# Pointwise products and forward row transform of the spectral layers, split into halves of 64 stationary columns

## What is computed

```python
def _spectral_conv(x, w1, w2):
    xf = jnp.fft.rfft2(x).reshape(Bb, G, WID, Hh, Wf)
    lo = jnp.einsum('bgixy,gioxy->bgoxy', xf[:, :, :, :M1, :M2], w1c)
    hi = jnp.einsum('bgixy,gioxy->bgoxy', xf[:, :, :, Hh - M1:, :M2], w2c)
    ...
    return jnp.fft.irfft2(out_ft.reshape(Bb, G * WID, Hh, Wf), s=(Hh, Ww))
h = _gconv1x1(h, fc0_w, fc0_b)
for i in range(4):
    h1 = _spectral_conv(h, sp_w1[i], sp_w2[i])
    h2 = _gconv1x1(h, w_w[i], w_b[i])
    h = h1 + h2
    if i < 3:
        h = _gswish(h, betas[i])
h = _gswish(_gconv1x1(h, fc1_w, fc1_b), betas[3])
return _gconv1x1(h, fc2_w, fc2_b)
```

## Time and profile before

| | |
|---|---|
| median of 3 runs | 3073.56 us |
| the profiled execution | 3098.2 us, its span 3096.2 us |
| mean granted TensorE clock | 0.92 of full speed |
| TensorE busy (matmul) | 2572.4 us, 83% of the span |
| TensorE weight loads busy | 1994.0 us, 64% |
| VectorE / ScalarE / GpSimd busy | 1935.2 / 1290.9 / 1026.9 us |
| the layers | from 1110 to about 2440 us of the span |

### The profile page before, as it was taken

How to read it: one execution, slowest core, us unless ns; L and a number is a source line. 1 busy time by engine, 2 the same in 40 slices (tenths; PEclk the granted TensorE clock), 3 DMA queues, 4 the chain that set the end, 5 groups by cost and what they waited for, 6 DMA issues and landing times. The chain is left out here.

```text
span 3096.2 us, 46908 instructions
## 1 busy us (share of the span) xinstructions
PE 2572.4 (83%) x18156; PEld 1994.0 (64%) x18156; DVE 1935.2 (63%) x2352; ACT 1290.9 (42%) x2167; POOL 1026.9 (33%) x1050
## 2 busy tenths in 40 slices
PE   0499999685978768999899989898987599999468
PEld 0144444343655457888888878788886488888345
DVE  4988876674852644346565656564754489898633
ACT  1687777463322321233233322233232377766322
POOL 1988810223621400202020101111111377777310
PEclk9999999897989889999998999998988799999789
DMA  8500002567522354589897989897987553551134
GB/s 185 118 0 26 0 26 47 164 182 165 131 54 79 104 100 131 181 215 234 203 240 194 225 198 216 227 215 222 210 215 194 130 98 71 81 102 21 62 99 105
DMA packets 242226, 423.46 MB, mean 137 GB/s; under 512 B 85930, under 2 KB 188970, under 8 KB 217154
## 3 DMA queue, kind: packets, MB, share of 16 engines
q1 hardware_dynamic: 218011, 381.07, 51.4%
q10 hardware_dynamic: 23520, 34.61, 3.8%
q0 software_dynamic: 496, 5.01, 0.4%
HBM read 252.61 MB, written 166.38 MB: 135 GB/s over the span
## 5 line engine op out<-in xcount | busy, mean ns | idle before, releaser
L1589 ACT ACTIVATE fno_act<-fno_pz 128x320 f32<-128x320 f32 x512 | 220.7, 438 | 722.2 <-PE fno_pz L1505 566.6
L1248 DVE STREAM_TRANSPOSE spec_chan<-spec_form_in 128x1024 f32<-128x1024 f32 x256 | 497.6, 1958 | 8.3 <-PEq L238 8.3
L1452 POOL TENSOR_SCALAR fno_xm<-fno_xm 40x384 f32<-40x384 f32 x96 | 114.3, 1190 | 992.4 <-DMA fno_xm<-scratch_modes 992.4
L1505 PE MATMUL fno_pz<-spec_cols,spec_chan 128*128 128x96 f32 x3072 | 395.7, 289 | 8.4 <-issue 8.4
L1505 PEld LDWEIGHTS fno_pz<-spec_cols,spec_chan 128*128 128x128 f32 x3072 | 380.9, 204 | 23.5 <-issue 19.6
L1879 POOL TENSOR_TENSOR head_hact_lo<-head_hact,head_hact_hi 128x512 fp32r<-128x512 f32 x256 | 343.7, 1366 | 136.6 <-DVE head_hact_hi L2021 136.6
L1535 PE MATMUL fno_pw<-fno_fw,fno_act 128*128 128x96 f32 x2560 | 310.9, 281 | 32.6 <-DVE fno_wfreq L1727 25.0
L1535 PEld LDWEIGHTS fno_pw<-fno_fw,fno_act 128*128 128x128 f32 x2560 | 300.6, 196 | 42.0 <-DVE fno_wfreq L1727 32.9
L611 PE MATMUL cml_acc<-cml_logis,cml_mats 128*128 128x512 f32 x480 | 246.8, 596 | 55.9 <-DVE cml_logis L568 55.9
L613 PE MATMUL cml_acc<-cml_moved,cml_mats 128*128 128x512 f32 x480 | 246.2, 594 | 11.2 <-ACT cml_moved L534 11.2
L1717 DVE COPY spec_cols<-fno_pj 48x512 f32<-48x512 f32 (+1 forms) x150 | 88.3, 604 | 222.2 <-PE fno_pj L1515 190.9
(11 more groups left out here) (224 smaller groups left out, 4806.9 us busy)
## 6 DMA issues: line engine op xcount, KB each, us to landing
scratch_form<-fno_act SPq DMA_DIRECT2D x32, 2560.0 KB
spec_form_in<-scratch_form SPq DMA_DIRECT2D x64, 1024.0 KB
fno_wt<-table_mix_w SPq DMA_DIRECT2D x192, 150.0 KB
fno_coef<-scratch_mixed SPq DMA_DIRECT2D x50, 480.0 KB, 9.4
nca_raw<-scratch_xnp SPq DMA_DIRECT2D x66, 329.7 KB
spec_form_in<-scratch_form SPq DMA_DIRECT2D x32, 512.0 KB
scratch_mixed<-fno_om ACTq DMA_DIRECT2D x96, 160.0 KB
scratch_mixed<-spec_om ACTq DMA_DIRECT2D x96, 160.0 KB
```

Of the source, the lines that this page charges most:

```text
L1248: return nc.vector.transpose(chan[:, to * TR * PIX:(to + 1) * TR * PIX].rearrange("p (h q w) -> p h q w", h=TR, q=4), src)
L1505: mm = nc.tensor.matmul(pz[:, t % 4, m * 96:(m + 1) * 96], left, cols[:, h * CS:h * CS + 96] if layer else wz[:, :], start=m == 0, stop=Tr ...
L1589: nc.scalar.activation(act_b[:, :, 4 * t:4 * t + 4], z, ACT.Silu if n >= UNITS else ACT.Copy).then_inc(a_out, 1)
```

## The change

Each of the two products becomes two, one for each half of the stationary columns. The halves' results go to PSUM partitions 0 to 63 and 64 to 127 of the same bank, where they lay before. The moving table is the same for both halves. For `pointwise` a half is one image of the pair (`B2` = 2, `W` = 64); for `forward_cols` it is one channel (`H` = 64). Nothing else changes: not the order, the waits, the buffers or the other engines' code.

```diff
-                        mm = nc.tensor.matmul(pz[:, t % 4, m * 96:(m + 1) * 96], left, cols[:, h * CS:h * CS + 96] if layer else wz[:, :],
-                                              start=m == 0, stop=True, skip_group_check=True)
+                        for b in range(B2):
+                            mm = nc.tensor.matmul(pz[W * b:W * b + W, t % 4, m * 96:(m + 1) * 96], left[:, W * b:W * b + W],
+                                                  cols[:, h * CS:h * CS + 96] if layer else wz[:, :],
+                                                  start=m == 0, stop=True, skip_group_check=True)
                     mm.then_inc(z_done, 1)
...
-                            mm = nc.tensor.matmul(pw[:, t % 2, m * 2 * SB:(m + 1) * 2 * SB],
-                                                  act_b[:, c0:c0 + 2, :].rearrange("p c h -> p (c h)"),
-                                                  fw[:, :], start=m == 0, stop=True, skip_group_check=True)
+                            for i in range(2):
+                                mm = nc.tensor.matmul(pw[H * i:H * i + H, t % 2, m * 2 * SB:(m + 1) * 2 * SB], act_b[:, c0 + i, :],
+                                                      fw[:, :], start=m == 0, stop=True, skip_group_check=True)
                         mm.then_inc(w_done, 1)
```

## The result

The changed kernel takes 3068.68 us (median of 20 runs, 3057.73 to 3087.22), the kernel before 3085.04 beside it (20 runs, 3072.54 to 3103.17). The ratio is 0.9946, 95% interval 0.9929 to 0.9962: some 17 us faster, or 0.5%. The forecast was 39 us. The profiled execution took 3057.73 us. What one trace says in single us is read with that in mind; verdicts go by medians.

What follows compares the result with a forecast made beforehand. TensorE, waiting for weight loads, was taken as the bound, with DMA engines also near their limit. Plain units 24 us saved, mixing units 6 lost, layer 0 21 saved: 39 us off, 3073.56 to 3035 us; range 2955 to 3115.

Steps and rivals of the forecast that it cites:

- Fetching in plain units: Plain units of layers 1 to 3: late instruction packets during the groups cost 1.5 us a unit.
- The pace of the halves: Both split products: a pair of half records takes 0.085 us, so a group falls from 0.89 to 0.68 us.
- the forward steps: Forward transform in plain units: only first and last two steps count, 1.0 us saved; the others wait for VectorE.
- layer 0: Layer 0's eight units, bound by the store: 12 groups after its landing get faster, 21 us saved.
- halves take turns: Rival, both products: a half's load and columns run one after the other, 0.28 us a product, 3220 us; chance 4%.
- the rule weighed ahead: Skill rule on TensorE: weight loads overlap a running matmul only in different row groups, so the change would lose.
- The forecast spacing of 24 us: Sign of being right: layer 0 units some 24 us apart, against 27.2 us between stores before.
- Plain units: 12 units of layers 1 to 3 without mixing: 2.0 us saved a unit after fetching, 24 us together.
- Mixing units: 12 units of layers 1 to 3: late packets lengthen the mixing stretch; 0.5 us lost a unit, 6 together.
- instructions come in time: Rival, TensorE's instruction fetch: stops have another cause or packets are called for earlier; 2940 us, chance 15%.
- fetching becomes the bound: Rival, mixing units above all: every packet could take 8.6 us, 77 us slower, 3150 us; chance 15%.
- transfers take it all: Rival, DMA: stores, unit loads and mixing weights keep the units' ends where they were, 3073 us; chance 8%.

Runs made afterwards that it cites:

- f_only: Changed kernel with the pointwise products left whole, so only the forward transform is split: 3070.77 us, ratio 0.9944 to the kernel before.
- z_only: Changed kernel with the forward transform left whole, so only the pointwise products are split: 3057.77 us, ratio 0.9907 to the kernel before.
- before_move: Kernel before, with ScalarE storing a mixing unit's last two mixed pieces behind its copies into `cols`: 3069.87 us, ratio 0.9934 to the kernel before.
- after_move: Changed kernel, with ScalarE storing a mixing unit's last two mixed pieces behind its copies into `cols`: 3027.58 us, ratio 0.9804 to the kernel before.
- pad: Changed kernel with a wait on a long-reached semaphore ahead of each half product: 3089.98 us, ratio 1.0013 to the kernel before.
- one part alone: Only the pointwise products split, the forward transform as in the kernel before: 3057.77 us, ratio 0.9907.
- before_pad: Kernel before with five waits on a long-reached semaphore ahead of each product of both kinds: 3145.5 us, ratio 1.0187 to the kernel before.

## Why the prediction was right and wrong

**The steps that failed.** Two terms of the sum did. Fetching in plain units, priced at 1.5 us a unit, cost 2.6. And the wait of the inverse rows behind ScalarE's store issues, 22.1 us in the trace of before, was put at nothing: it grew by half, and with the stores moved the change is worth 42 us where it is worth 17 without. The pace of the halves, the forward steps and layer 0 came out as forecast.

**The pace: right.** A group takes 0.69 us for the 0.68 forecast. The 0.085 us for a pair of halves fits, and that halves take turns is refuted. The Trainium skill has a rule that fits this too (TensorEngine Tiling (Array Packing), Key Properties): different tiles load weights and multiply in parallel. The trace agrees, with 0.69 us a group, and disagrees with the rule weighed ahead (TensorE: Matmul & The Clock Gate, Part 3).

**The forward steps: right.** 0.92 us a plain unit in f_only (9.76 to 8.84 from the first to the last matmul of the transform) for the 1.0 forecast, and the rest is waiting for VectorE as said: 34.0 us in 42 waits in the changed kernel, for 9.2 in 22 before.

**Layer 0: near.** 271.2 to 252.0 us, 19 for 21, in the profiled pair, although four stops at packets' ends with 12.3 us came there, for which the sum had no term. The forecast spacing of 24 us stands twice in z_only (24.0), where one such stop is left.

**Plain units: the first step that failed.** The undisturbed unit saves 3.7 us, where the sum had 3.5 before fetching. The term "1.5 for fetching" was sized by the excess of the stops in the mixing units of the kernel before. The table gives it directly: the mean unit lies 31.68 - 28.5 = 3.2 us above the undisturbed one, where it lay 32.83 - 32.2 = 0.6 before, so fetching costs 2.6 a unit more, not 1.5; the stops alone are 2.4, where these units had none before. The saving is 1.15 a unit for 2.0, or 14 us for 24. Two things were left out of the size. Behind a stop of several us groups can run at half the granted clock (2.62 us for 1.5 in the timeline above). And the forward transform's split adds to the stops in the groups: plain units have 2.4 us of them for 0.9 in z_only. More packets run out there, 41 for 34; but those that last under 6.2 us are 10 for 9, and the next one lands after 6.4 us in the mean, for 4.9. Why it lands later is open.

**Mixing units: right in sum by luck, wrong in the way; here the second step failed.** They last as long as before (49.82 for 49.70; 0.5 more was forecast). The sum priced only the stretch with the mixing pieces, and took what it gained or lost to the unit's end. Behind it stands a wait that was in the trace of before and was priced nowhere: the inverse rows, for ScalarE's copies behind its store issues. TensorE that comes earlier waits there longer: the stretch with the mixing pieces was to get 1.4 us longer, and the groups got 0.8 us shorter, the inverse rows 1.8 longer. Two errors cancel. Moving the stores gave 18 us before and 41 after, so some 23 us of gain lay there. That the change then gives 42 us, near the 39 of the sum, is luck too: between before_move and after_move the table has 24 us from layer 0, 6 from plain units and 21 from mixing units, where the sum had 21, 24 and a loss of 6.

**What doesn't add up in one trace.** By the profiled pair, the layers' 31 units gained 30 us, against 37 of the forecast; by the medians the gain is 17. The forecast was also set on a median of three runs, 3073.56, where 20 give 3085.04: 12 us of its distance to the time come from there, and none of the missing gain. Between the 30 us of the pair and the 17 of the medians no trace decides.

**The rivals.** That instructions come in time is what the light loads show, in which the change gives 108 us; at full load it isn't so. That fetching becomes the bound did not come: 32 of 113 packets end in a stop, of 3.5 us in the mean. That transfers take it all is half of the truth: 17 us did reach the end, but the transfers delay the packets.

**Open** is what in the traffic delays a packet, what the 21 us of pad are, and how much of the gain with light loads is the packets' alone, as they ease every transfer at once.

## What to carry to other kernels

Splitting a product into halves that load and stream side by side pays where the weight load sets the pace, but it doubles the instructions; where transfers are dense, compare how long a packet of instructions lasts with how long the next one takes to land. Before forecasting a faster stretch, look for the wait that ends it already: a small one in the profile of before (22 us here) takes up the gain until what stands ahead in the other engine's queue is moved. Measure the parts of a change alone as well as together: here one part alone gave 29 us and both together 17.

## What was not expected of the hardware

- A long stop for instructions costs again behind its end: behind the stop of 5.73 us the granted clock was 0.50, and two groups took 2.62 us instead of 1.5; behind the stop of 3.11 us it was 1.00 (from 1526.6 to 1529 us). The Trainium skill (Runtime: NRT & Kernel Launch, Instruction fetch mechanics) calls the crossing of a 16 KB boundary mostly hidden; the 32 stops with 113.2 us of this kernel disagree.
- ScalarE's issues of stores differ: two (of `fno_om`) in 0.68 us at one time, three (of `spec_om`) in 3.70 us and four in 5.65 at another.

```profile
1462.08 0.68 ACTq L1619 DMA_DIRECT2D scratch_mixed<-fno_om  x2
```

- Waits for a semaphore that was reached long ago can be nearly free of instructions: in pad 6656 waits, one ahead of each half product, made 535 instructions, and two groups of halves kept their 1.49 us. In before_pad five ahead of each of 3328 products made 7191.

```profile
1490.40 1.49 PE L1507 MATMUL fno_pz<-spec_cols,spec_chan 128*64 128x96 f32 x32
```
